# One expert's weights per tile of 128 token slots, with the tokens sorted by expert first, in place of masks over all experts

## The chip, the cores and the metric

The kernel runs on one core of a Trainium2 chip. The metric is device time in microseconds (us), of one launch. The kernel has two parts, one behind the other: attention over 8 sequences (not touched here), and a layer of experts over the same 4,096 tokens.

## The reference, cut to what matters

`x` is the normalised output of the attention, 4,096 rows of 256. There are 8 experts, each token uses the 2 with the highest router value, and the state goes through 2 iterations. (The biases, `mu`, the router and the halting gate are left out of the excerpt where they say nothing new.)

```python
topk_p, topk_i = jax.lax.top_k(probs, K)            # K = 2 of E = 8
v = jnp.zeros_like(xf)
integrated = xf
for _ in range(ITERS):                              # 2
    ctx = jnp.concatenate([integrated, v], axis=-1) # 512 wide
    shared_ctrl = _gelu(ctx @ shared_w1 + shared_b1) @ shared_w2 + shared_b2
    x_sh, v_sh = _inl(shared_ctrl, integrated, v, mu)
    ctrl = _experts(ctx_e, flat_idx, expert_w1, expert_b1, expert_w2, expert_b2)
    x_r, v_r = _inl(ctrl, x_e, v_e, mu)             # one row for each token-expert pair
    ...
    x_next = sw * x_sh + (1.0 - sw) * x_r           # x_r, v_r: weighted sum of the 2 pairs
    v_next = sw * v_sh + (1.0 - sw) * v_r
    halt = jax.nn.sigmoid(_gelu(integrated @ halt_w1 + halt_b1) @ halt_w2 + halt_b2)
    integrated = integrated + halt * (x_next - integrated)
    v = v + halt * (v_next - v)
refined = _gelu(integrated @ refine_w1 + refine_b1) @ refine_w2 + refine_b2
out = layernorm(xf + integration_weight * refined)

def _inl(ctrl, xs, vs, mu):
    a, b, g = jnp.split(ctrl, 3, axis=-1)           # ctrl is 768 wide
    v_next = jax.nn.sigmoid(a) * vs - jax.nn.softplus(b) * (xs - mu)
    return xs + 0.1 * jax.nn.sigmoid(g) * v_next, v_next
```

An expert has a hidden width of 64: 512 -> 64 -> 768. In the first iteration `v` is zero, so only half of the first product and two thirds of the second are needed.

## The kernel before, in words

`experts` works on groups of 512 tokens (4 tiles of 128), 8 groups, two at a time in flight. A stage is one iteration of one group: kinds 1 and 2 are the two iterations, kind 3 is the refinement and the normalisation. A hardware loop runs stages in the order written in `ROUND`: (2, 0), (2, 1), (3, 0), (1, 0), (3, 1), (1, 1), where the second number is the group of the pair. So iterations and refinements of different groups lie beside each other all the time. Every engine has its own instruction stream, and the streams wait for each other on semaphores.

Numbers are kept in float32 precision by splitting each operand in two float16 parts, high and low, and by three products (`split_products`, L1688 to L1690).

In a stage of kind 1 or 2, TensorE turns the state (L1677), computes the router and halting layer (L1728) and the hidden layers of **all** 8 experts and the shared one, for all 512 tokens. One-hot rows of the two chosen experts are spread by TensorE to masks (L1719), and VectorE multiplies the hidden values of all experts by the mask of the first and of the second choice (L1536, `routed`). `control` (L1782) then computes the 768 control values for each tile of 128 tokens and each of 3 streams (the shared expert, the first choice, the second choice). A routed stream takes 13 products over the whole width of 512 hidden values (1 for the bias, 3 for each of 4 chunks), the shared one 2.

ScalarE takes the result out of PSUM: tanh (L1361) and relu (L1363), and later a logarithm (L1348), for which it switches its table and switches back (L1343, L1351). GpSimd makes two products of 128x768 for each tile (L1289, L1291), and VectorE does the rest of `_inl` and the weighted sum (L1544, L1553 to L1569), again for each tile with its 3 streams.

SyncE issues all transfers; in this part they are the weights, the state of each group and the result of each group.

The names that the prediction uses: `control`, `tanhs`, `softplus_logs`, `update`, `low_parts`, `refine_hidden`, `refine_out`, `take_refined`, `refine_variance`, `finish`.

## Time and profile before

| | us |
|---|---|
| median of 3 runs | 1670.16 (1669.14 to 1681.21) |
| the profiled execution: its time | 1671.22 |
| its span | 1669.5 |
| attention, to the first instruction of `experts` at | 594 |
| TensorE busy in the span | 1355.1 (81%) |
| VectorE | 1121.7 (67%) |
| ScalarE | 827.3 (50%) |
| GpSimd | 518.6 (31%) |

The profile's page gives first the busy time of each engine, then the share of busy time in 40 slices, the queues of the transfers, the chain of work that ended last, and the costliest groups of instructions. Attention is the first 14 slices. A matmul's listed duration is its way through a pipeline; what it costs in a row of matmuls is the distance from its start to the start of the next one.

### The profile page before, as it was taken

Reading aid. Unit: us, or ns where it says so; the run is one execution under the profiler, and the core shown is the slowest. Engines: PE = TensorE matmul, PEld = TensorE weight load, DVE = VectorE, ACT = ScalarE, POOL = GpSimd, SP = SyncE. Lnnn points to the kernel's source line nnn. Section 1 sums busy time; section 2 is a strip of 40 time slices with the busy share of each in tenths; the row PEclk is TensorE's granted clock in tenths of the full one; section 3 lists DMA queues with packets and bytes.
Section 4 is the critical chain, followed back from the end, with each engine's and each line's share of the span. In section 5 each row is a group of like instructions: output and inputs, shape, how many; then the busy total and the mean of one; then the engine's idle time right before and its main releaser. Section 6 shows DMA issues by size and latency. Waiting matters only on the chain.

```text
span 1669.5 us, 22624 instructions
## 1 busy us (share of the span) xinstructions
PE 1355.1 (81%) x7776; PEld 726.9 (44%) x7776; DVE 1121.7 (67%) x2038; ACT 827.3 (50%) x1429; POOL 518.6 (31%) x490
## 2 busy tenths in 40 slices
PE   4778877888889827889978789988789987789964
PEld 2334543545445413345533345543345543345532
...
GB/s 83 154 66 122 48 94 105 56 121 56 85 111 19 26 153 1 1 0 1 3 12 26 1 15 1 1 13 26 1 15 1 1 13 11 16 13 1 1 0 26
DMA packets 83216, 62.54 MB, mean 37 GB/s; under 512 B 27633, under 2 KB 82185, under 8 KB 83090
## 3 DMA queue, kind: packets, MB, share of 16 engines
...
q14 instruction: 55, 0.45, 0.1%
...
## 4 chain that ended last, share of the span: by engine, by line
PE 36%; DVE 16%; ACT 5%; issue 4%; SPq 1%; POOL 1%; DMA 1%; POOLq 0%; DVEq 0%; ACTq 0%
PE exp_ps L1782 19%; DVE x L1569 5%; PE exp_ps L1688 4%; PE exp_ps L1690 4%; PE exp_ps L1689 4%; DVE ctrl L1558 2%; PE exp_ps L1677 2%; DVE onehot L1488 2%; PE exp_ps L1728 1%; ACT gp L1338 1%; SPq L1141 1%; PE exp_ps L1719 1%; DVE top_f L1484 1%; DVE sp L1556 1%; DVE ctrl L1553 1%
## 5 line engine op out<-in xcount | busy, mean ns | idle before, releaser
L1782 PE MATMUL exp_ps<-w,routed 128*128 128x512 f16 (+1 forms) x2304 | 442.2, 346 | 1.6 <-DVE routed L1536 1.6
L1289 POOL TENSOR_TENSOR sp<-sp,ctrl 128x768 f32<-128x768 f32 x64 | 124.5, 1945 | 645.4 <-ACT ctrl L1348 645.4
L1782 PEld LDWEIGHTS exp_ps<-w,routed 128*128 128x128 f16 x2304 | 226.7, 99 | 199.8 <-issue 12.2
L563 DVE TENSOR_REDUCE neg_max<-att_ps 128x1 f32<-128x512 f32 (+3 forms) x448 | 216.9, 533 | 71.4 <-PE att_ps L732 69.5
L501 ACT ACTIVATE probs<-att_ps 128x512 f32<-128x512 f32 x320 | 175.5, 609 | 168.3 <-PE att_ps L741 167.3
L1361 ACT ACTIVATE ctrl<-exp_ps 128x512 f32<-128x512 f32 (+1 forms) x192 | 137.2, 715 | 195.3 <-PE exp_ps L1782 194.8
L731 PE MATMUL att_ps<-k_stack,q_stack 96*128 96x512 bf16 (+3 forms) x512 | 161.1, 356 | 69.8 <-DVE neg_max L563 32.5
L1544 DVE TENSOR_SCALAR ctrl<-ctrl 128x768 uint32<-128x768 uint32 x64 | 67.9, 1061 | 125.9 <-ACT ctrl L1361 125.8
L1569 DVE SCALAR_TENSOR_TENSOR x<-ctrl,nwx,x 128x256 f32<-128x256 f32 x192 | 145.7, 759 | 3.4
L741 PE MATMUL att_ps<-q_stack,k_stack 98*128 98x512 bf16 (+3 forms) x512 | 124.6, 317 | 8.3 <-DMA q_stack<-max_parts 5.8
L732 PE MATMUL att_ps<-mask_q,identb 128*128 128x128 bf16 x512 | 125.5, 251 | 0.0
L1291 POOL TENSOR_TENSOR sp<-sp,xm 128x768 f32<-128x768 f32 x64 | 120.8, 1887 | 5.0
L731 PEld LDWEIGHTS att_ps<-k_stack,q_stack 96*128 96x128 bf16 x512 | 54.2, 109 | 143.0 <-DVE neg_max L563 93.9
L1677 PE MATMUL exp_ps<-e_ident,x 128*128 128x128 f32 x192 | 34.4, 330 | 90.2 <-DVE x L1569 56.1
L408 POOL TENSOR_TENSOR wait_carrier<-wait_carrier 128x1 f32<-128x1 f32 x64 | 12.3, 193 | 294.6 <-ACT probs L501 294.6
L1536 DVE TENSOR_TENSOR routed<-gp,masks 128x1024 f16<-128x1024 f16 x128 | 82.8, 688 | 17.3 <-ACT masks L1389 13.9
L1336 ACT ACTIVATE g<-exp_ps,b 128x512 f32<-128x512 f32 x80 | 54.9, 686 | 79.6 <-PE exp_ps L1690 79.5
L413 POOL TENSOR_SCALAR_AFFINE_SELECT probs<-probs 128x640 f32<-128x640 f32 (+2 forms) x192 | 86.6, 483 | 0.0
L1558 DVE SCALAR_TENSOR_TENSOR ctrl<-ctrl,sp 128x768 f32<-128x768 f32 x64 | 76.9, 1202 | 1.1
L798 PE MATMUL att_ps<-probs,values 128*32 128x512 f32 (+3 forms) x1024 | 76.1, 436 | 1.4 <-issue 1.4
L1363 ACT ACTIVATE sp<-exp_ps 128x256 f32<-128x256 f32 x192 | 75.8, 395 | 0.0
L1677 PEld LDWEIGHTS exp_ps<-e_ident,x 128*128 128x128 f32 x192 | 26.2, 168 | 101.8 <-issue 48.9
...
## 6 DMA issues: line engine op xcount, KB each, us to landing
...
x_in<-in_L_attn_encodings SPq DMA_DIRECT2D x8, 512.0 KB, 10.6
normed_dram<-normed SPq DMA_DIRECT2D x8, 512.0 KB, 11.2
x<-normed_dram SPq DMA_DIRECT2D x8, 512.0 KB, 3.9
out<-final SPq DMA_DIRECT2D x8, 512.0 KB, 2.9
ctrl<-in_L_ffn_expert_w SPq DMA_DIRECT2D x1, 1536.0 KB, 8.4
```

The lines of the kernel that those rows point to most:

```text
L501: nc.scalar.activation(probs[:, pair % 4, u, :], src, ACT.Exp).then_inc(free, 1)
L563: return v.tensor_reduce(out, scores, AX.X, ALU.max, negate=True)
L731: t_.matmul(out, stationary, moving, start=True, stop=False)
L732: return t_.matmul(out[:, at:at + P], identb[:], mask, start=False, stop=True)
L741: return t_.matmul(out, k_stack[p][:, h, i * P:(i + 1) * P], q_stack[p][:, h, i * P:TOK], start=True, stop=True)
L1289: gp_.tensor_tensor(sp[:, t], sp[:, t], ctrl[:, t, :, D:2 * D], ALU.subtract).then_inc(pool_step, 1)
L1291: gp_.tensor_tensor(sp[:, t], sp[:, t], xm[:, t, :].unsqueeze(1).to_broadcast([P, STREAMS, D]), ALU.mult).then_inc(spx_ready, 1)
L1361: nc.scalar.activation(ctrl[:, t, s, cols], ctrl_ps(s)[:, 0:width], ACT.Tanh, scale=0.5).then_inc(tanh_done, 1)
L1558: v.scalar_tensor_tensor(gg, gg, 1.0, sp[:, t], ALU.add, ALU.mult).then_inc(update_step, 1)
L1569: last = v.scalar_tensor_tensor(x_new, ctrl[:, t, s, 2 * D:], nwx[g][:, t, s:s + 1], src[g][:, t, :] if s == 0 else x_new, ALU.mult, ALU.add)
L1677: last = t_.transpose(dst[:, t * P:(t + 1) * P], src[:, t, c * P:(c + 1) * P], ident[:])
L1782: last = t_.matmul(ctrl_ps(s)[:, a - cols[0][0]:z - cols[0][0]], stationary, moving[:, a:z], start=(j == 0), stop=(j == len(terms) - 1))
```

## The change

Only `experts` is replaced. What it does now, in the order of its phases:

1. The setup loads all 8 groups' rows at once and keeps the state of all 4,096 tokens in SBUF (`xs`, `vs`). For each group, the router and the shared hidden layer of iteration 1 are computed.
2. The shared expert's control values of iteration 1 (8 groups, units `W_S1`). Beside them: the two choices of each token give 8,192 pairs; VectorE computes for each pair its place in the order of experts, each expert's part padded to whole tiles of 128 slots, 72 tiles (`SLOTS`) in all, 18 units of 4 tiles (`QUADS`). GpSimd scatters each row of `xs` to two places of a DRAM tensor `xs_dram` (64 indirect transfers of 128 rows), which SyncE has filled with zeros before (18 transfers).
3. Iteration 1 of the pairs in 18 units (`W_B`): a unit's rows are loaded from `xs_dram`, each tile uses one expert's weights, whose place TensorE takes from a register that it loads from `tile_expert` (`quad_experts`). The results go to DRAM (`rs1_dram`, 1 MB a unit).
4. Iteration 2 of the shared expert in 8 groups (`W_S2`). Ahead of each, 8 indirect transfers gather the two result rows of each token (`gather1`), and `combine1` adds them to the state. The new state goes to DRAM (`xv_dram`).
5. Iteration 2 of the pairs in 18 units (`W_D`), their rows gathered from `xv_dram` (`gather_state`, 72 indirect transfers of 128 rows of 2 KB), the results stored to `rs2_dram`.
6. The refinement and normalisation of 8 groups, each after 8 indirect transfers (`gather2`) and `combine2`.

A unit has 4 tiles of one stream. `ct` and `rb` have two halves, used in turn (`n % 2`). A routed tile takes 7 products of 128 columns for its hidden layer in iteration 1 and 13 in iteration 2, and 2 products for its control values (the second one carries the low parts and the bias). The diff, cut (`+` of the new kernel, `-` of the old one where it is shown):

```diff
+        GROUPS = SEQS
+        TILES = GROUPS * NT
+        QUADS = 18
+        SLOTS = QUADS * NT
+        XW = D + 4
+        CBW = 2 * 2 * D
+        CBS, CB2S = 6, 8
...
+            sync.wait_ge(zeros_ready, 1)
+            for q in range(QUADS):
+                sync.dma_start(quad_rows(xs_dram, q), zeros[:].unsqueeze(1).to_broadcast([P, NT, XW])).then_inc(pads_zero, 16)
...
+            def load_sorted(q):
+                if q == 1:
+                    sync.wait_ge(ctrl_filled[1], uses(W_B) // 2)
+                if q >= 3:
+                    sync.wait_ge(ew_done, W_B + q - 3 + 1)
+                load(xg_it1(q), quad_rows(xs_dram, q), xg_full[q % 3])
+            def store_results(n, dram, q, width):
+                sync.wait_ge(ew_done, n + 1)
+                sync.dma_start(quad_rows(dram, q), rb[:, n % 2, :, 0:width]).then_inc(rs_stored[n % 2], 16)
+            for g in range(GROUPS):
+                sync.wait_ge(scattered[g], 16 * 2 * NT)
+            for q in range(3):
+                load_sorted(q)
+            for q in range(QUADS):
+                store_results(W_B + q, rs1_dram, q, 2 * D)
+                if q + 3 < QUADS:
...
+            pool.wait_ge(late_in, 16 * LATE)
...
+            pool.wait_ge(pos_ready, 1)
+            pool.wait_ge(pads_zero, 16 * QUADS)
+            for t in range(TILES):
+                for k in range(2):
+                    g_.indirect_dma_start(xs_dram, IndirectOffsetOnAxis(pos[:, 2 * t + k:2 * t + k + 1], 0),
+                                          xs[:, t, :], None).then_inc(scattered[t // NT], 16)
+            def products(n, x):
+                par = n % 2
+                b = ct[:, par, :, D:2 * D] if it_of(n) == 2 else ct[:, par, :, 0:D]
+                m = rb[:, par, :, D:]
+                pool.wait_ge(ln_done, n + 1)
+                g_.tensor_tensor(m, m, b, ALU.subtract).then_inc(pool_step, 1)
+                pool.wait_ge(pool_step, n - W_B + 1)
+                g_.tensor_tensor(m, m, x, ALU.mult).then_inc(mul_done, 1)
+            for q in range(QUADS):
+                products(W_B + q, xg_it1(q)[:, :, 0:D])
+            def gather1(t):
+                if t >= CBS:
+                    pool.wait_ge(comb_done, t - CBS + 1)
+                for k in range(2):
+                    g_.indirect_dma_start(cb1(t)[:, k, :], None, rs1_dram,
+                                          IndirectOffsetOnAxis(pos[:, 2 * t + k:2 * t + k + 1], 0)
+                                          ).then_inc(cb_full[t % CBS], 16)
+            pool.wait_ge(ew_done, W_S2)
+            for i in range(2):
+                pool.wait_ge(rs_stored[i], 16 * stores_before(W_S2, i))
+            for t in range(2 * NT):
+                gather1(t)
+            for g in range(GROUPS):
+                for t in range((g + 2) * NT, min((g + 3) * NT, TILES)):
+                    gather1(t)
+                products(W_S2 + g, xs[:, g * NT:(g + 1) * NT, 0:D])
+            def gather_state(q):
+                if q >= 3:
+                    pool.wait_ge(ew_done, W_D + q - 3 + 1)
                 for t in range(NT):
...
+            for q in range(3):
+                gather_state(q)
+            for q in range(QUADS):
+                products(W_D + q, xg_it2(q)[:, :, 0:D])
+                if q + 3 < QUADS:
+                    gather_state(q + 3)
...
+            def tanhs(n):
+                par, it = n % 2, it_of(n)
+                if n >= 2:
+                    act.wait_ge(ew_done, n - 2 + 1)
+                    if is_shared(n - 2):
+                        act.wait_ge(acc_done, shared_before(n - 2) + 1)
+                    else:
+                        act.wait_ge(rs_stored[par], 16 * (stores_before(n - 2, par) + 1))
+                for u in range(uses(n), uses(n + 1)):
+                    act.wait_ge(ctrl_filled[u % 2], u // 2 + 1)
+                    i = u - uses(n)
+                    if it == 1:
+                        raw = slot_ps(u).rearrange("p (t n) -> p t n", t=2)
+                        last = s.activation(ct[:, par, 2 * i:2 * i + 2, 0:2 * D], raw, ACT.Tanh, scale=0.5)
+                        if u == uses(n + 1) - 1:
+                            last.then_inc(tanh_done, 1)
+                        s.activation(rb[:, par, 2 * i:2 * i + 2, D:], raw[:, :, 0:D],
+                                     ACT.Relu).then_inc(ctrl_freed[u % 2], 1)
+                    else:
+                        raw = slot_ps(u)[:, 0:CTRL]
+                        last = s.activation(ct[:, par, i, :], raw, ACT.Tanh, scale=0.5)
+                        if u == uses(n + 1) - 1:
+                            last.then_inc(tanh_done, 1)
+                        s.activation(rb[:, par, i, D:], raw[:, D:2 * D], ACT.Relu).then_inc(ctrl_freed[u % 2], 1)
+            def logs(n):
+                par = n % 2
+                b = ct[:, par, :, D:2 * D] if it_of(n) == 2 else ct[:, par, :, 0:D]
+                s.preload_act_table_set("natural_log_exp_and_others")
+                act.wait_ge(abs_done, n + 1)
+                s.activation(b, b, ACT.Ln, scale=0.5, bias=half[:, 0:1]).then_inc(ln_done, 1)
+                s.preload_act_table_set("gelu_and_others")
+            act.wait_ge(rf_stored, 32)
+            act.wait_ge(w2_ready, 1)
...
+            def absolute(n):
+                par = n % 2
+                b = (ct[:, par, :, D:2 * D] if it_of(n) == 2 else ct[:, par, :, 0:D]).bitcast(U32)
+                dve.wait_ge(tanh_done, n + 1)
+                v.tensor_scalar(b, b, 0x7FFFFFFF, None, ALU.bitwise_and).then_inc(abs_done, 1)
+            def velocity(n, vel):
+                par = n % 2
+                a, gg, m = ct[:, par, :, 0:D], ct[:, par, :, 2 * D:], rb[:, par, :, D:]
+                dve.wait_ge(mul_done, n - W_B + 1)
+                v.scalar_tensor_tensor(a, a, 1.0, vel, ALU.add, ALU.mult).then_inc(dve_step, 1)
+                then()
+                v.scalar_tensor_tensor(m, a, -10.0, m, ALU.mult, ALU.add).then_inc(dve_step, 1)
+                then()
+                v.scalar_tensor_tensor(rb[:, par, :, 0:D], gg, 1.0, m, ALU.add, ALU.mult).then_inc(ew_done, 1)
...
+            def add_shared1(g):
+                n = W_S1 + g
+                dve.wait_ge(ew_done, n + 1)
+                dve.wait_ge(scattered[g], 16 * 2 * NT)
+                for t in range(NT):
+                    tt = g * NT + t
+                    v.scalar_tensor_tensor(xs[:, tt, 0:D], rb[:, n % 2, t, 0:D], nwx[0][:, tt, 0:1], xs[:, tt, 0:D],
+                                           ALU.mult, ALU.add)
+                    last = v.tensor_scalar(vs[:, tt, :], rb[:, n % 2, t, D:], nwx[0][:, tt, 0:1], None, ALU.mult)
+                last.then_inc(acc_done, 1)
...
+            def combine1(g):
+                for t in range(g * NT, (g + 1) * NT):
+                    dve.wait_ge(cb_full[t % CBS], 32 * (t // CBS + 1))
                     for k in range(2):
...
+            for g in range(GROUPS):
+                if g + 1 < GROUPS:
+                    lows("c", g + 1, 2 * KC)
+                absolute(W_S2 + g)
+                weigh(g)
+                if g + 2 < GROUPS:
+                    combine1(g + 2)
+                if g:
+                    velocity(W_S2 + g - 1, vs[:, (g - 1) * NT:g * NT, :])
+                    add_shared2(g - 1)
+                if g + 1 < GROUPS:
+                    hidden(W_S2 + g + 1, f"cs{g + 1}", h_hl, h_h1)
...
+            for q in range(QUADS):
+                if q + 1 < QUADS:
+                    lows("d", q + 1, 2 * KC)
+                absolute(W_D + q)
+                if q:
+                    velocity(W_D + q - 1, xg_it2(q - 1)[:, :, D:])
+                if q + 1 < QUADS:
+                    hidden(W_D + q + 1, f"dh{q + 1}", h_hl, h_h1)
+            velocity(W_D + QUADS - 1, xg_it2(QUADS - 1)[:, :, D:])
...
+            for g in range(GROUPS):
+                if g:
+                    lows("e", g, KC)
+                    steps = spread_of(g - 1)
+                refine_low(g)
+                if g:
+                    finish(g - 1, steps)
+                take(g)
+                if g + 2 < GROUPS:
+                    combine2(g + 2)
+            finish(GROUPS - 1, spread_of(GROUPS - 1))
         @block.tensor
         def _(pe):
             t_ = nc.tensor
...
+            def control_tile(dst, it, hl, h1, w_at):
+                parts = ((0, 2 * D), (2 * D, CTRL)) if it == 2 else ((D, CTRL),)
+                for j, (stationary, moving) in enumerate(((hl, w2_top), (h1, w2_low))):
+                    for a, z in parts:
+                        last = t_.matmul(dst[:, a - parts[0][0]:z - parts[0][0]], stationary,
+                                         moving[:, ds(w_at + a, z - a)], start=(j == 0), stop=(j == 1))
+                return last
...
-                    else:
-                        k = s - 1
-                        terms = [(onehotT[g][:, k, tok], b2_parts[:])]
-                        for c in range(EC):
-                            terms += [(routed[:, k, 0, c, tok], w2[:, 0, c, :]),
-                                      (routed[:, k, 0, c, tok], w2[:, 1, c, :]),
-                                      (routed[:, k, 1, c, tok], w2[:, 0, c, :])]
-                    for j, (stationary, moving) in enumerate(terms):
...
+            def quad_experts(q):
+                return [pe.value_load(tile_expert[0:1, q * NT + i:q * NT + i + 1], min_val=0, max_val=E - 1)
+                        for i in range(NT)]
+            def routed_hidden(name, chunks, es):
+                dst, done = ring(name)
+                flat = w1[:].rearrange("p a c e r h -> p a c (e r h)")
+                for i in range(NT):
+                    tok = slice(i * P, (i + 1) * P)
+                    o = dst[:, tok]
+                    for c in range(chunks):
+                        hi, lo = flat[:, 0, c, ds(es[i] * P, P)], flat[:, 1, c, ds(es[i] * P, P)]
+                        t_.matmul(o, hi, xT[:, 0, c, tok], start=(c == 0), stop=False)
+                        t_.matmul(o, hi, xT[:, 1, c, tok], start=False, stop=False)
+                        t_.matmul(o, lo, xT[:, 0, c, tok], start=False, stop=False)
+                    last = t_.matmul(o, b1_parts[:, ds(es[i] * P, P)], ones[:], start=False, stop=True)
+                last.then_inc(done, 1)
+            def turn_sorted1(q):
+                pe.wait_ge(xg_full[q % 3], 16 * (q // 3 + 1))
...
+            for q in range(QUADS):
+                if q + 1 < QUADS:
+                    turn_sorted1(q + 1)
+                control(W_B + q, h_hl, h_h1, offsets(es))
+                if q + 1 < QUADS:
+                    es = quad_experts(q + 1)
+                    ready("b", q + 1, KC)
+                    routed_hidden(f"bh{q + 1}", KC, es)
```

## Rows read from the trace of the kernel before

**Rows 1.** Busy time by stretch: attention, experts, the end (header: the columns)

```profile
core 0: us, PE busy (x) PEld busy (x) DVE busy (x) ACT busy (x) POOL busy (x), PEclk, DMA share, GB/s
0.00:594.00 594.00, 470.89 (x3216) 261.26 (x3216) 344.18 (x776) 244.90 (x451) 167.78 (x298) 0.89 0.51 81
594.00:1628.00 1034.00, 866.61 (x4480) 456.04 (x4480) 762.95 (x1217) 569.44 (x958) 339.60 (x187) 0.92 0.04 13
1628.00:1669.50 41.50, 17.58 (x80) 9.65 (x80) 14.61 (x46) 12.96 (x20) 11.20 (x5) 0.66 0.08 26
```

**Rows 2.** Waits, 800 to 1600 us: who waited for whom, total, times, longest

```profile
POOL sp L1289 <- ACT ctrl L1348: 537.8, 26, 30.9
ACT ctrl L1361 <- PE exp_ps L1782: 160.5, 75, 3.2
```

**Rows 3.** Groups by shape, from 740 us: busy us, mean ns; idle before, releaser

```profile
L1782 PE MATMUL exp_ps<-w,routed 128*128 128x512 f16 x1344 | 390.8, 384 | 0.9 <-DVE routed L1536 0.9
L1782 PE MATMUL exp_ps<-w,routed 128*128 128x256 f16 x768 | 209.4, 273 | 0.0
...
L1361 ACT ACTIVATE ctrl<-exp_ps 128x768 f32<-128x768 f32 x96 | 78.6, 819 | 116.1 <-PE exp_ps L1782 116.0
L1363 ACT ACTIVATE sp<-exp_ps 128x256 f32<-128x256 f32 x168 | 66.2, 394 | 0.0
...
L1348 ACT ACTIVATE ctrl<-ctrl,half 128x768 f32<-128x768 f32 x58 | 51.1, 928 | 0.3
L1336 ACT ACTIVATE g<-exp_ps,b 128x512 f32<-128x512 f32 x67 | 46.0, 686 | 71.2 <-PE exp_ps L1690 71.1
L1527 DVE TENSOR_TENSOR gp<-g,gp 128x512 f16<-128x512 f32 x55 | 37.9, 690 | 25.7 <-ACT gp L1338 25.5
L1343 ACT ACT_TABLE_LOAD x29 | 37.2, 1283 | 0.5
L1280 POOL TENSOR_TENSOR xm<-x,mu 128x1024 f32<-128x1024 f32 x14 | 33.3, 2376 | 1.2
L1318 ACT CAST xTp<-exp_ps 128x512 f16<-128x512 f32 x42 | 25.5, 608 | 0.0
```

**Rows 4.** Timeline of VectorE and GpSimd, side by side and alone: start, us

```profile
1077.73 0.96 DVE L1558 SCALAR_TENSOR_TENSOR ctrl<-ctrl,sp 128x768 f32<-128x768 f32 x1
1077.78 2.57 POOL L1289 TENSOR_TENSOR sp<-sp,ctrl 128x768 f32<-128x768 f32 x1 [8.23 <-ACT ctrl L1348]
1078.72 5.81 DVE L1569 SCALAR_TENSOR_TENSOR x<-ctrl,nwx,x 128x256 f32<-128x256 f32 x3
1091.08 1.52 DVE L1569 SCALAR_TENSOR_TENSOR x<-ctrl,nwx,x 128x256 f32<-128x256 f32 x3
```

**Rows 5.** Timeline of TensorE: the same work at either clock, and 128 columns

```profile
1042.07 0.38 PE L1688 MATMUL exp_ps<-xTp,w 128*128 128x512 f16 x1
1042.29 0.38 PE L1689 MATMUL exp_ps<-xTp,w 128*128 128x512 f16 x1
...
1628.11 1.97 PE L1677 MATMUL exp_ps<-e_ident,x 128*128 128x128 f32 x8 [11.99 <-DVE x L1569]
1633.15 0.63 PE L1689 MATMUL exp_ps<-xTp,rf 128*128 128x512 f16 x1
1633.58 0.64 PE L1690 MATMUL exp_ps<-xTp,rf 128*128 128x512 f16 x1
...
441.61 0.22 PE L731 MATMUL att_ps<-k_stack,q_stack 96*128 96x128 bf16 x1
441.66 0.22 PE L732 MATMUL att_ps<-mask_q,identb 128*128 128x128 bf16 x1
```

**Rows 6.** Transfers: median us to landing; then one issue on SyncE's queue

```profile
out<-final SPq DMA_DIRECT2D x8, 512.0 KB, 2.9
ctrl<-in_L_ffn_expert_w SPq DMA_DIRECT2D x1, 1536.0 KB, 8.4
...
609.84 0.43 SPq L1141 DMA_DIRECT2D ctrl<-in_L_ffn_expert_w  x1
```

1589 lines of the change are left out of this document (840 added, 749 removed).

## The prediction

> **What bounds the kernel now.** I read the busy time by stretch first. Experts take 1034 us plus 41.5 us at the end, 1075 of 1669.5; attention, untouched, 594. In the 1034 us TensorE is busy 866.6 us (84%) at a granted clock of 0.92, VectorE 763 (74%), ScalarE 569 (55%), GpSimd 340 (33%) [rows 1]. The waits say the same: GpSimd waits for ScalarE's logarithm, 537.8 us, and ScalarE for TensorE's control products, 160.5 us [rows 2]. By shape, those products are the dearest group (390.8 and 209.4 us listed) and never wait for data [rows 3]. So TensorE is the bound, with VectorE close behind: relief on TensorE alone can't give more than about 1034 - 763 = 271 us.
>
> **What is removed.** Control products fall from 2688 (28 terms a tile, one piece of 512 columns in iteration 1, pieces of 512 and 256 in iteration 2) to 624. Starts of 512 columns are 0.22 us apart at the high clock, 0.43 at the low [rows 5], so it is 481 against 112 us at the high clock. Hidden layers: 720 products of 512 columns (155 us) become 144 of 512 and 1440 of 128 columns, the latter 0.055 us apart (bf16 rows of attention) [rows 5]: 110 us. Masks go, with VectorE's multiplications by them (128 x 0.69 us = 88 us). TensorE loses some 430 us and stops being the bound.
>
> **What isn't removed.** tanh, relu, logarithm and `_inl`: before 32 tiles x 3 streams x 2 = 192 stream-tiles; now 2 x (32 + 72) = 208, because of padding. I therefore cost each phase by the loop that its waits close. Prices for 128x1024 (4 tiles at once): ScalarE 1.0 us from PSUM (0.82 for 768, 0.39 for 256), 0.6 for 512, logarithm 1.15 (0.93 for 768), a table switch 1.28, a GELU 0.6 from start to start, a cast 0.5 [rows 3]; VectorE 1.2 us (0.96 for 768), 0.5 for 256 columns [rows 4], 0.69 for a low part [rows 3]; GpSimd 2.38 [rows 3].
>
> Two prices are chosen. **Contention:** three VectorE instructions on 256 columns take 1.52 us alone, 5.81 us beside GpSimd's products: one gets through per GpSimd instruction [rows 4]. So a pair of products (4.7 us) costs VectorE up to 4.7 us, if two-input work of VectorE falls on it. **An indirect transfer on GpSimd, c:** before has none. The nearest rows are an issue on SyncE, 0.43 us [rows 6], and a GpSimd instruction over 128x1024, 2.38 us [rows 3]. I take the middle, c = 1.4 us for 128 rows. Landing: 2.9 us for 512 KB, 8.4 for 1536 KB [rows 6], so 5.7 for 1 MB and 2.5 for a small one.
>
> **Phase 1, setup and routing, 594 to 768.** VectorE's first low part waits for all late weights. About 10 MB are ahead of that wait; 1.5 MB in 8.4 us is 183 GB/s [rows 6], less its fixed part 200: 50 us, to 645. The first group then carries, in one chain, TensorE 6, ScalarE's cast of 6,912 columns 6, VectorE's low parts of them 8, the ones, bias and refine splits 11, its own hidden layer, turning and routing 14: 45, to 690. Seven more groups: router 3.4 and shared product 2.6 at the low clock, turning 2.0 [rows 5], cast and low part 1.5; between 6.5 and 10.5, I take 8.5: 60. Gates, one-hots, first control and rank products 6, prefix sums and slots (some 35 VectorE instructions of 0.2 to 0.7) 12: 768. The zeros for 9.6 MB take 50 us of transfers, under the routing.
>
> **Phase 2, scatter, to 860.** 64 c = 90 us, 2.5 landing. The shared control units lie under it (VectorE 7.9 a group, 63 in all): `add_shared1` waits for its group's scatter, as it writes the rows that are read. What covers VectorE's work here is the scatter; at small c the 63 us remain.
>
> **Phase 3, 18 units of iteration 1, to 1115.** Load 4 and fill 15. Loop: from one unit's GELU, `hidden` on VectorE 1.0, control of two tiles 1.7 (low clock), 3.2 for tanhs (the second slot comes 1.7 later), switch 1.28, logarithm 1.15, switch 1.28, GELU 1.2: 11.1. `hidden` of the next unit falls on GpSimd's products (they start with the end of the logarithm, last 4.7): plus 2.3 = 13.4; 12.3 at the high clock. I take 13: 17 x 13 = 221. The store (1 MB, 5.7) that `tanhs` two units later waits for gives 11.3, just beneath. Tail 15: logarithm, products, velocity, store.
>
> **Phase 4, iteration 2 of the shared expert, to 1321.** Nothing of it starts before phase 3's last store. First tanhs end after 37: 16 gathers 22.4 + 2.5, combine, turning, 18 products, GELUs, control. Then VectorE is the loop: magnitude 0.9, weights 0.4, `combine1` of 16 instructions 8.2, velocity 3.6, `add_shared2` 2.0, `hidden` 1.0, contention 4, then 7.1 in which it waits for turning, control and four tanhs: 27.2. GpSimd needs 8 c + 4.7 = 16 and hides. 7 x 27.2 less 22 (two groups without combine, one without velocity) = 168; total 206.
>
> **Phase 5, 18 units of iteration 2, to 1621.** Start 37 (logarithm, products, 4 c, turning at the low clock, 52 products, GELU, control). Loop: the gather of 3 units ahead waits for this unit's velocity and stands before the next unit's products, on which the next velocity waits: 3.6 + 4 c + 4.7 + 0.9 contention + 0.2 = 15.0. ScalarE's own loop is 11 to 13.6. What is queued behind GpSimd's wait is thus the products, and VectorE's velocity behind them. 17 x 15 less 6 for the last units = 249, tail 14.
>
> **Phase 6, refinement, to 1856.** First take after 39 (gathers 13.7, turning, 24 and 48 products mostly at the low clock). Before, each refinement lay beside another group's iteration; now a group's is one chain: GpSimd's two products 4.7 with 1 of delay, `combine2` finishing late through contention (to 10 us after `take`), low parts 1.3, variance 2.0, root and switch 1.7, four pairs of GELUs 5.5, low part 0.7, 39 products of 256 columns 4.3: 26. The end of before shows it: from turning at 1628.11 to the span's end is 41 us for one such chain and a half, TensorE at clock 0.66 [rows 1, 5]. 7 x 26 = 182, tail 14.
>
> **The sum:** 594 + 174 + 92 + 255 + 206 + 300 + 235 = 1856 us of span, against 1669.5. The profiled execution's time is 1671.22 and the median 1670.16, 1 us above the span: 1857. So 430 us of TensorE work go, and phases that no longer lie beside each other, their fills, and 264 indirect transfers take more.
>
> No transfer of this trace is issued by GpSimd, so c rests on its two neighbours [rows 3, 6]. The Trainium skill ("DMA: Bandwidth & Descriptors", Anatomy of one DMA, SWDGE path) calls descriptor generation on GpSimd "small, variable", beside about 50 ns of dispatch; by it the sum would be near the first two rivals, 1569 to 1755, by the rows' middle it is 1857. No run here bears the rule out yet.
>
> **Rivals.** (1) *Indirect transfers are nearly free, and ScalarE bounds every loop: faster, 1569.* With c = 0.45 as SyncE's issue, the high clock and no contention: phase 1 150; phase 2 65 (VectorE); phase 3 15 + 170 + 12; phase 4 25 + 7 x 19 less 8; phase 5 30 + 17 x 11 + 12; phase 6 30 + 7 x 20 + 14. That is 975, with attention 1569. For it: the lower price row. Against: the low clock after each idle stretch (8 transposes in 1.97 us) and the contention rows [rows 4, 5]. It decides when the phases behind attention come under 1060 us; c alone can't do it, since it moves at most 64 + 16 + 68 + 8 = 156 us per us, and only down to where ScalarE's loop holds phase 5. (2) *Cheap transfers, else as forecast:* c = 0.75: 1857 - 0.65 x 156 = 1755. (3) *Dear transfers:* c = 2.38: 1857 + 153 = 2010. (4) *TensorE bounds the routed loops.* Each unit loads 4 registers from SBUF between its control and its hidden products, and addresses go through them. No row shows a price: 0 to 1 us each, the latter twice SyncE's issue. Phase 5's TensorE loop at the low clock is 13.6 + 4 loads, above 15 from 0.35 us a load; at 1 us 17.6, phase 3's 15: 17 x (2.6 + 2) = 78, 1935. (5) *The change doesn't do what it says* (an expert overfull, more tiles than 72) is excluded: 8192 pairs need at most 64 + 8 tiles.
>
> **Chances.** Forecast (1790 to 1900) 0.45; (1) 0.07; (2) 0.17; (3) 0.12; (4) 0.17; 0.02 left for no change. A measurement of this kernel tells about 1% from no change. Faster by over 1% 0.07, within 1% 0.02, slower 0.91. The range reaches to most of (2) and half of (3): 1725 to 1985, leaving out (1) and the dear end.
>
> **What would show it.** Right: in the trace after, TensorE's busy share of experts under 60% and a clock under 0.8; four phases with GpSimd's queue filled by transfers; phase 5's units 15 us apart, with the products' wait released by VectorE; refinement groups 26 us apart; nothing routed before 645. Wrong: c far from 1.4; VectorE's instructions of equal length beside GpSimd's products; fills shorter than 30 us.

## The result: 16% slower, and the profile after

The changed kernel takes 1940.25 us (median of 4 runs, 1933.24 to 1948.69) against 1672.58 us (1669.14 to 1681.21) beside it: a ratio of 1.159, 95% interval 1.153 to 1.166. The forecast was 1857 with a range of 1725 to 1985. The time lies inside, 83 us above 1857. That is one phase missed by 95 us, while the errors of the others (19 us too little, 32 too much) go against each other. The profiled execution's span is 1938.2 us, and it is divided below at the forecast's own marks.

First the page of the profile after: busy time of each engine (share of the span, instructions), then the granted clock in 40 slices, in tenths.

```profile
PE 1109.8 (57%) x6930; PEld 680.5 (35%) x6930; DVE 1021.0 (53%) x1930; ACT 870.4 (45%) x1339; POOL 718.1 (37%) x699
...
PEclk9588998989896566657667767766877777767778
```

No engine is busy over 60%. TensorE was at 81% of the span and 1355 us before; it has lost only 245 us of busy time, not the 430 of the forecast's high-clock price. Most of that gap is the clock, which went from 0.9 to 0.759: busy time times granted clock, added up by stretch behind attention, falls by some 355 us (an estimate from [rows 1] and the rows below). The same by stretch, with marks taken from GpSimd's timeline (attention, 594 us, left out); the columns are those of [rows 1]:

```profile
594.00:766.00 172.00, 73.74 (x258) 38.00 (x258) 68.69 (x204) 47.40 (x69) 32.24 (x33) 0.62 0.44 123
766.00:855.00 89.00, 21.02 (x48) 5.91 (x48) 53.98 (x92) 48.86 (x51) 67.92 (x64) 0.58 0.27 96
855.00:1121.00 266.00, 124.20 (x792) 82.60 (x792) 112.88 (x133) 158.37 (x197) 80.89 (x34) 0.71 0.31 100
1121.00:1341.00 220.00, 104.92 (x464) 61.60 (x464) 160.61 (x264) 97.77 (x154) 108.98 (x83) 0.69 0.38 124
1341.00:1714.00 373.00, 205.93 (x1512) 166.35 (x1512) 147.28 (x186) 200.98 (x305) 152.06 (x106) 0.75 0.24 74
1714.00:1938.00 224.00, 108.83 (x640) 65.47 (x640) 133.07 (x278) 71.95 (x113) 108.29 (x82) 0.75 0.28 86
```

One stretch stands out: 1341 to 1714, the 18 routed units of iteration 2. TensorE is busy 55% of it, ScalarE 54%, GpSimd 41%, VectorE 39%. Where [rows 1] had one engine at 84%, here a loop through several engines sets the pace. Who waits in it (waits of the experts' part, 594 to 1938 us: total, times, longest):

```profile
POOL rb L1296 <- ACT ct L1452: 306.8, 29, 23.8
ACT e_xT L1389 <- PE exp_ps L1917: 294.6, 102, 27.1
POOL xg L1327 <- DVE rb L1721: 165.9, 15, 12.5
PE exp_ps L1917 <- DMA xg<-xs_dram: 114.8, 15, 8.0
PE exp_ps L1917 <- DMA xg<-xv_dram,ids: 109.8, 16, 18.6
```

Read the last three together. GpSimd's gather (L1327) waits 15 times for the velocity (L1721) that frees its buffer. Then TensorE's transposes (L1917) wait for the gather's landing, 16 times. The line above shows the same for iteration 1, with SyncE's load in the gather's place. In the view of the kernel before that [rows 2] is taken from, 50 rows long, no wait is on a transfer.

**Forecast and marks, phase by phase.** All marks are starts on GpSimd's queue; "forecast" and "measured" give the stretch's end, and "difference" compares the lengths.

| phase | forecast | measured | difference |
|---|---|---|---|
| 1: setup and routing, to the first scatter | 594 to 768 | 594 to 766.6 | -1 |
| 2 and 3: scatter, 18 units, to the first gather of results | to 1115 | to 1132.8 | +19 |
| 4: shared control, iteration 2, to the first gather of state | to 1329 (1321, then the last logarithm and products) | to 1340.8 | -6 |
| 5: 18 units, to the next gather of results | to 1621 | to 1727.7 | +95 |
| 6: refinement | to 1856 | to 1938.2 | -25 |

### The profile page after: what moved, and what is told of

The parts are those of the page before. It is cut to its first block, busy times and chain, and to the rows that moved or that the text cites. A ratio compares the mean times of both kernels' runs of the same rounds, so it can differ in the third digit from the quotient of the medians.

```text
span 1938.2 us, 21725 instructions
## 1 busy us (share of the span) xinstructions
PE 1109.8 (57%) x6930; PEld 680.5 (35%) x6930; DVE 1021.0 (53%) x1930; ACT 870.4 (45%) x1339; POOL 718.1 (37%) x699
## 4 chain that ended last, share of the span: by engine, by line
DVE 19%; PE 14%; ACT 11%; DMA 10%; issue 9%; POOL 5%; SPq 2%; POOLq 0%; ACTq 0%; DVEq 0%
PE exp_ps L1917 5%; DMA xg<-xs_dram 5%; PE exp_ps L1939 4%; ACT ct L1442 3%; DMA xg<-xv_dram,ids 3%; POOL xg L1327 2%; ACT ct L1435 2%; DVE xs L1847 2%; DVE xs L1781 2%; DVE vs L1782 2%; DVE ct L1710 2%; DVE rb L1721 2%; PE exp_ps L1989 1%; DVE rb L1719 1%; SPq L1122 1%
## 5 line engine op out<-in xcount | busy, mean ns | idle before, releaser
L1917 PE MATMUL exp_ps<-e_ident,xg 128*128 128x128 f32 x432 | 95.0, 405 | 253.2 <-DMA xg<-xs_dram 114.8
L1389 ACT CAST e_xT<-exp_ps 128x512 f16<-128x512 f32 x172 | 97.7, 591 | 295.2 <-PE exp_ps L1917 294.6
L1296 POOL TENSOR_TENSOR rb<-rb,ct 128x1024 f32<-128x1024 f32 x44 | 106.3, 2416 | 307.1 <-ACT ct L1452 306.8
L1551 DVE TENSOR_TENSOR e_xT<-exp_ps,e_xT 128x512 f16<-128x512 f32 x172 | 115.1, 689 | 136.5 <-ACT e_xT L1389 135.7
L1917 PEld LDWEIGHTS exp_ps<-e_ident,xg 128*128 128x128 f32 x432 | 82.8, 216 | 259.7 <-DMA xg<-xs_dram 117.2
L2030 PE MATMUL exp_ps<-e_xT,w 128*128 128x128 f16 x432 | 108.9, 262 | 53.1 <-issue 52.9
L1327 POOL DMA_INDIRECT xg<-xv_dram,ids x72 | 71.4, 991 | 183.1 <-DVE rb L1721 165.9
L1939 PE MATMUL exp_ps<-w_top,h_hl 128*128 (+2 forms) x280 | 102.2, 430 | 37.5 <-DVE h_hl L1558 22.1
L2032 PE MATMUL exp_ps<-e_xT,w 128*128 128x128 f16 x432 | 108.3, 261 | 0.0
L2031 PE MATMUL exp_ps<-e_xT,w 128*128 128x128 f16 x432 | 107.8, 260 | 0.0
L1939 PE MATMUL exp_ps<-w_low,h_h 128*128 (+2 forms) x280 | 98.5, 416 | 0.0
L1442 ACT ACTIVATE ct<-exp_ps 128x768 f32<-128x768 f32 x104 | 84.4, 812 | 13.3 <-PE exp_ps L1939 10.4
L1917 PE MATMUL exp_ps<-e_ident,xs 128*128 128x128 f32 x192 | 32.4, 325 | 99.4 <-DVE vs L1782 68.5
```

Source lines behind the costliest of these rows:

```text
L1327: g_.indirect_dma_start(xg_it2(q)[:, t, :], None, xv_dram, IndirectOffsetOnAxis(ids[:, q * NT + t:q * NT + t + 1], 0)).then_inc(gx_full[q ...
L1442: last = s.activation(ct[:, par, i, :], raw, ACT.Tanh, scale=0.5)
L1551: v.tensor_tensor(xT[:, 1, c, :], ps[:, n % RINGS, :], xT[:, 0, c, :], ALU.subtract).then_inc(ring_freed[n % RINGS], 1)
L1917: last = t_.transpose(dst[:, t * P:(t + 1) * P], tiles(t), ident[:])
L1939: last = t_.matmul(dst[:, a - parts[0][0]:z - parts[0][0]], stationary, moving[:, ds(w_at + a, z - a)], start=(j == 0), stop=(j == 1))
L2030: t_.matmul(o, hi, xT[:, 0, c, tok], start=(c == 0), stop=False)
```

## One unit of phase 5 in the trace after

The unit takes 20.4 us from one pair of products to the next (forecast 15.0). Timeline of the kernel after, one unit, by start; repeated rows left out. Columns: start us, duration us, engine, line, what, and in brackets the idle time before it and what ended it.

```profile
1468.85 1.22 DVE L1721 SCALAR_TENSOR_TENSOR rb<-ct,rb 128x1024 f32<-128x1024 f32 x1
...
1470.34 0.99 POOL L1327 DMA_INDIRECT xg<-xv_dram,ids  x1 [10.85 <-DVE rb L1721]
...
1471.63 0.95 POOL L1327 DMA_INDIRECT xg<-xv_dram,ids  x1 [0.30 <-issue]
...
1473.67 0.69 DVE L1558 TENSOR_TENSOR h_hl<-g,h_hl 64x512 f16<-64x512 f32 x1
1474.13 1.05 POOL L1327 DMA_INDIRECT xg<-xv_dram,ids  x1 [0.30 <-issue]
1475.20 2.35 POOL L1296 TENSOR_TENSOR rb<-rb,ct 128x1024 f32<-128x1024 f32 x1
...
1478.35 3.38 PE L1917 MATMUL exp_ps<-e_ident,xg 128*128 128x128 f32 x16 [6.13 <-DMA xg<-xv_dram,ids]
...
1481.57 0.49 PE L1939 MATMUL exp_ps<-w_top,h_hl 128*128 x2
...
1482.50 0.81 ACT L1442 ACTIVATE ct<-exp_ps 128x768 f32<-128x768 f32 x1
...
1486.40 0.69 DVE L1710 TENSOR_SCALAR ct<-ct 128x1024 uint32<-128x1024 uint32 x1 [3.29 <-ACT ct L1442]
...
1487.01 1.22 DVE L1717 SCALAR_TENSOR_TENSOR ct<-ct,xg 128x1024 f32<-128x1024 f32 x1
```

`hidden`'s low parts are ready at 1474.36, and the control products that use them start only at 1481.57. In between TensorE stands before `turn_sorted2` of the next unit, for 6.13 us, until that unit's gather has landed. That gather could start only after the velocity at 1468.85 to 1470.07. So the loop is: velocity, buffer free, four transfers (1470.34 to 1475.2), landing (1478.35), turning (3.4, at the low clock), control, tanhs (1482.50 to 1486.37), magnitude, velocity (to 1490.75). The working had the gather ahead of the products, which is so (GpSimd's products start at 1475.20). But it let the next velocity wait for those products, and they end at 1479.98, 7 us before that velocity starts: VectorE has the next unit's magnitude (1486.40) ahead of it, and this waits for the tanhs. What the working did not have is the landing and the turning ahead of the control products: it took "3 units ahead" as slack, and one of the three is being turned while another is computed.

## Experiments

Two parts of this reading could fail: another wait might close the same loop, or the loop might be TensorE's own, as the forecast's rival (4) has it. That rival's time, 1935, is nearly the measured one. The first scatter, up to which all the changed kernels run the same code, lies anywhere from 758 to 777 us in their profiled executions, so small differences between medians are read from marks and units inside the traces. **Summary**, differences against the kernel after (1940.25) or, where named, against e9 (1825.26):

| kernel | median us | ratio to before, 95% | difference |
|---|---|---|---|
| e1 seven buffers, phase 5 | 1844.68 | 1.099 to 1.110 | -96 |
| e2 control ahead of turning, phase 5 | 1890.47 | 1.127 to 1.133 | -50 |
| e3 five buffers, phase 3 | 1918.25 | 1.140 to 1.151 | -22 |
| e4 half of the scatter | 1934.72 | 1.152 to 1.163 | -6 |
| e6 no GpSimd products in phase 3 | 1933.56 | 1.152 to 1.159 | -7 |
| e7 buffers and order, both phases | 1899.88 | 1.132 to 1.142 | -40 |
| e8 the same without register loads | 1889.89 | 1.127 to 1.132 | -10 to e7 |
| e9 buffers in both phases | 1825.26 | 1.090 to 1.095 | -115 |
| e10 e9 without register loads | 1826.11 | 1.090 to 1.095 | +1 to e9 |
| e11 e9 with register loads earlier | 1836.78 | 1.092 to 1.102 | +12 to e9 |
| e12 e9 without GpSimd products in phase 3 | 1769.49 | 1.055 to 1.060 | -56 to e9 |
| e5 kernel before, fewer control products | 1604.82 | 0.957 to 0.962 | -67 to before |

### The landing: e1, e3, e9

e1 gives phase 5 seven buffers instead of three (four lie in `vs`, free by then), so a gather runs units ahead of its turning:

```diff
+            if q % 7 >= 3:
+                return view(vs_flat, (q % 7 - 3) * 2048, NT, 2 * D)
...
-                    pool.wait_ge(ew_done, W_D + q - 3 + 1)
+                    pool.wait_ge(ew_done, W_D + max(q - 7 + 1, 0))
```

> Seven buffers in place of three for the rows gathered in iteration 2 (the four new ones lie in vs, which is free by then). Theory A (the buffer's return closes the loop: in the changed kernel's trace a unit's gather waits for the velocity of the unit three before, lands about 8 us later, and only then TensorE turns it, in front of the control products of the unit before): with more buffers nothing waits for the return, a unit goes from 20.5 us to 13.5 to 15, 17 x 6 = 100 us less, about 1840. Theory B (TensorE bounds the unit, by its register loads and the low clock, 13.6 us + 4 loads): a unit stays at 18 us or more, at most 45 us less. Theory C (the rate of the transfers: 4 gathers of 256 KB and a store of 512 KB a unit): no change.

Measured 1844.68, 96 us less. The waits of e1 from 1372 to 1720 us no longer hold a wait of L1919 (there the line of the transposes) on a transfer. In phase 5 the profiled executions, from the first gather of state to the last products, take 373.3 us after and 277.7 in e1, so the 95.6 us between them are the whole miss of that phase. The turning gains too: 16 transposes take 1.94 us in e1 where they took 3.38 behind the wait.

The unit is 14.45 us (products at 1478.48, 1492.95, 1507.41 in e1's timeline) where the forecast had 15.0. The numbers are near, but the loop is another one. GpSimd, whose queue the forecast's 15.0 follows, waits for ScalarE's logarithm in every unit of e1, and the last steps, 14.4 us each, have no gather in them at all:

```profile
POOL rb L1298 <- ACT ct L1454: 74.3, 17, 8.6
...
1575.08 0.95 POOL L1329 DMA_INDIRECT vs<-xv_dram,ids  x1 [0.30 <-issue]
1579.78 2.50 POOL L1298 TENSOR_TENSOR rb<-rb,ct 128x1024 f32<-128x1024 f32 x1 [3.75 <-ACT ct L1454]
...
1594.22 2.51 POOL L1298 TENSOR_TENSOR rb<-rb,ct 128x1024 f32<-128x1024 f32 x1 [8.62 <-ACT ct L1454]
...
1608.64 2.50 POOL L1298 TENSOR_TENSOR rb<-rb,ct 128x1024 f32<-128x1024 f32 x1 [8.62 <-ACT ct L1454]
```

In e1 the chain that repeats goes through TensorE: control products (1470.85 to 1474.82), 2.46 us of idle time, hidden products (1477.28), GELUs (1482.19), copy, low part, and the next control products at 1485.32.

e3 gives phase 3 five buffers for SyncE's load, as each there is half as large:

```diff
-            at = (q % 3) * 2064
+            at = (q % 5) * 1040
...
-                    sync.wait_ge(ew_done, W_B + q - 3 + 1)
+                    sync.wait_ge(ew_done, W_B + q - 5 + 1)
```

> Five buffers in place of three for the sorted rows of iteration 1, nothing else. Theory A: the same loop, through SyncE's load (issue to landing 6.0 us) in place of the gather: a unit goes from 14.4 us to 12.5 to 13, 17 x 1.7 = 29 us less, about 1911. Rival: contention of VectorE with GpSimd's products, or the store of 1 MB, closes the loop: no change within 10 us.

Measured 1918.25: 22 us less (phases 2 and 3 together take 347.2 us instead of 366.1). Units fall from 14.36 to 13.2 us; the forecast took 13. Two rows of the kernel after show what stood there: the load is issued when the velocity is done, and lands in front of the transposes.

```profile
991.65 0.51 SPq L1122 DMA_DIRECT2D xg<-xs_dram  x1
...
997.73 1.97 PE L1917 MATMUL exp_ps<-e_ident,xg 128*128 128x128 f32 x8 [7.49 <-DMA xg<-xs_dram]
```

e9 has both edits.

> The kernel after, with five buffers for phase 3's loads and seven for phase 5's gathers; order as in the kernel after. The landing theory: the two gains (95 and 22 us) stand in different phases and add, so about 1822 us (1812 to 1835). Rival: the two phases share something (a buffer, a queue), and the sum is 1835 to 1850.

Measured 1825.26, 115 us less: the two gains add, to within 3 us of the 118 that they make apart.

### Another order instead of more buffers: e2, e7

If landing and turning are ahead of the control products, one could let the control products go first. e2 does so in phase 5, on all three engines:

```diff
-                if q + 1 < QUADS:
-                    turn_sorted2(q + 1)
                 control(W_D + q, h_hl, h_h1, offsets(es))
                 if q + 1 < QUADS:
+                    turn_sorted2(q + 1)
```

and in the same way `casts` after `tanhs` on ScalarE and `lows` after `absolute` on VectorE.

> Three buffers as in the changed kernel, but in iteration 2 of the pairs the control products of a unit stand before the turning of the next one on TensorE, with the casts behind the tanhs on ScalarE and the low parts behind the magnitude on VectorE. Theory A: the gather may land late, since control no longer waits for it; a unit is then closed by velocity 3.7 + gathers 4.8 + products 4.8 + some waiting = 14 to 15 us, about 1840, within 20 us of the run with seven buffers. Theory B: 18 us or more a unit, above 1890. If buffers alone matter and not the order, no change.

Measured 1890.47: half of the gain, with units of 16.6 us, between what the two theories asked for. The expectation missed what the old order hid: in e2 the hidden products wait 2.83 us for low parts. e7 shows it with the landing out of the way (this order and the deep buffers in both phases):

> The changed kernel with seven and five buffers and with control before turning in both iterations of the pairs. Theory A: units of 11.5 to 13 us in iteration 1 and 12 to 14 in iteration 2: 1940 - 17 x 1.9 - 17 x 7.3 = 1784, between 1770 and 1820. It stays above the kernel before, since setup, scatter and the fills between the phases are not touched. Theory B: above 1850.

Measured 1899.88, 75 us more than e9 with the same buffers and 116 above the middle of what was expected. A unit of phase 5 takes 17.9 us in e7 against 14.45, one of phase 3 14.3 against 13.2. e7's timeline of one unit:

```profile
1466.99 0.82 PE L1941 MATMUL exp_ps<-w_top,h_hl 128*128 x2 [3.34 <-DVE h_hl L1560]
...
1468.57 0.81 ACT L1444 ACTIVATE ct<-exp_ps 128x768 f32<-128x768 f32 x1 [3.80 <-PE exp_ps L1941]
...
1472.82 2.06 ACT L1391 CAST e_xT<-exp_ps 128x512 f16<-128x512 f32 x4
1473.44 2.48 DVE L1553 TENSOR_TENSOR e_xT<-exp_ps,e_xT 128x512 f16<-128x512 f32 x4
1474.90 1.28 ACT L1452 ACT_TABLE_LOAD   x1
...
1476.28 0.23 PE L2032 MATMUL exp_ps<-e_xT,w 128*128 128x128 f16 x1 [2.73 <-DVE e_xT L1553]
```

The casts (2.06 us) now lie between the tanhs and the table switch, on ScalarE's chain, and the hidden products wait 2.73 us for low parts made behind them. In the old order both lay beside TensorE's idle time before the control products. So the wait that the order removed was the cover of other work, and what was late next was that work.

e7's unit of phase 5 is also 1.3 us longer than e2's, though it has more buffers. In e2 the gathers, which wait for the velocity, hold GpSimd's products back, and VectorE's copy of the hidden values (L1557) takes 0.29 us. In e7 the products start as the logarithm ends, and the same copy (L1559) takes 1.45 us beside them (means from 1400 to 1540 us).

### Register loads on TensorE, the forecast's rival (4): e8, e10, e11

Each unit has four `value_load` of expert numbers on TensorE between control and hidden products. In e1 TensorE is idle there, with nothing named:

```profile
1477.28 0.23 PE L2032 MATMUL exp_ps<-e_xT,w 128*128 128x128 f16 x1 [2.46 <-issue]
```

e8 and e10 take constants in their place, over e7 and e9; what they leave out is that each tile gets its own expert's weights:

```diff
-                return [pe.value_load(tile_expert[0:1, q * NT + i:q * NT + i + 1], min_val=0, max_val=E - 1)
-                        for i in range(NT)]
+                return [(q * NT + i) % E for i in range(NT)]
```

e11 keeps the loads and puts them ahead of turning:

```diff
+                this = offsets(es)
                 if q + 1 < QUADS:
+                    es = quad_experts(q + 1)
                     turn_sorted2(q + 1)
-                control(W_D + q, h_hl, h_h1, offsets(es))
+                control(W_D + q, h_hl, h_h1, this)
                 if q + 1 < QUADS:
-                    es = quad_experts(q + 1)
```

> As the run before it, but TensorE takes constants in place of the expert numbers loaded to registers (tile i uses expert i mod 8), so that each pair gets some expert's values and not its own: the register loads and computed addresses are gone. Theory A (hidden behind ScalarE's logarithm): within 15 us of the run before it. Theory B (they are on TensorE's path, about 2.5 us a unit as the trace of the changed kernel shows before L2030): 17 x 2 x 2.5 = 85 us less.

> As the kernel with both buffers deeper, and the experts' numbers are constants (slot tile i takes expert i mod 8), so TensorE loads no registers; the routed outputs are then of the wrong experts, by intent. In the trace with seven buffers TensorE stands 2.46 us idle, issue named, between the control products and the hidden products of every unit of phase 5, with nothing else late. Theory of the register loads: they are that gap and close the unit of 14.45 us, which falls to about 12; 17 units of 2.4 us less: about 1780 us (1770 to 1795). Rival: another engine closes the unit as soon (ScalarE is busy 10.9 us of it, VectorE 10.6), and less than 12 us come off.

> As the kernel with both buffers deeper, and TensorE loads the registers of the next unit ahead of turning it rather than behind this unit's control products; nothing is left out. TensorE waits 1.26 us for the low parts of the hidden sums there, so of 2.46 us of loads about 1.2 remain: 17 units of about 1.2 us less, about 1800 us (1793 to 1812). Rival (loads cost nothing): the same as with both buffers deeper within 5 us.

Measured: e8 1889.89 (10 us less than e7), e10 1826.11 (1 us more than e9), e11 1836.78 (12 more). As the price of a unit rival (4) is out: it asked for 78 us. The expectations of e10 (40 us less) and of e11 (25 less) both failed. The gap is gone in e10, and it lay on the chain that repeats in e1; but the unit of phase 5 grew from 14.45 to 15.35 us (15.1 and 15.6 in turn), while that of phase 3 fell from 13.2 to 13.1. One view says where the gain went: VectorE's groups by shape, 1400 to 1600 us (line, shape, count | busy, mean ns | idle before). In e1, whose phase 5 is built as e9's:

```profile
L1559 DVE COPY h_h<-h_hl 64x512 f16<-64x512 f16 x14 | 14.7, 1051 | 18.5 <-ACT h_hl L1406 18.5
```

In e10, and then in e11:

```profile
L1559 DVE COPY h_h<-h_hl 64x512 f16<-64x512 f16 x13 | 31.5, 2421 | 0.0
L1559 DVE COPY h_h<-h_hl 64x512 f16<-64x512 f16 x13 | 31.7, 2440 | 0.0
```

The copy needs 0.28 us alone. In e10 ScalarE's GELUs no longer wait for the hidden products (2.5 us in e1), so the copy starts 3.5 us after GpSimd's first product instead of 4.9, in the middle of the second, and is held until that ends: 1.05 us became 2.42. What the missing loads gave, contention took back. TensorE then waits 3.7 us for `hidden`, 2.4 more than in e1, and its granted clock from 1400 to 1600 us falls from 0.90 to 0.82.

e11's trace shows both at once, and its loss lies in phase 5 alone (301 us against 291 in e9, units of 14.4 to 15.4 us; phase 3 keeps its 13.2). The idle gap has moved with the loads and stands ahead of the transposes. And as ScalarE's GELUs no longer wait for hidden products there either, the copy is held as long as in e10, 2.44 us.

```profile
1438.13 3.17 PE L1919 MATMUL exp_ps<-e_ident,xg 128*128 128x128 f32 x16 [2.52 <-issue]
```

How the 10 us divide between the two was not separated.

### VectorE beside GpSimd's products: e6, e12

The forecast priced contention from [rows 4] and put 2.3 us of it into phase 3's unit. e6 takes GpSimd's two products of that phase over 4 of the 256 columns of each tile (16 of 1024 in a unit), in the kernel after; e12 does the same in e9. Both leave most of the routed velocities of iteration 1 unscaled:

```diff
+                if it_of(n) == 1:
+                    m, b, x = m[:, :, 0:4], b[:, :, 0:4], x[:, :, 0:4]
```

> The changed kernel with GpSimd's two products a unit in iteration 1 of the pairs on 4 of 256 columns, so that part of the result is left out: two instructions of 2.4 us become short. GpSimd is idle 9.7 us of each unit there. Theory E (contention: VectorE's h_hl instruction takes 2.73 us beside the products, 0.69 alone): it is 0.69 again and the time falls by up to 18 x 2.0 = 36 us, less if the landing of the load closes the loop instead (14.4 us a unit stays): 0 to 36. Rival (an idle engine's work is free): under 5 us, and the h_hl instruction stays at 2.7.

> As the kernel with both buffers deeper, and GpSimd's two products of a unit of phase 3 are taken over 4 columns of 1024, so most of the routed velocities of iteration 1 keep their unscaled values. With three buffers the landing of the load covered this. With five buffers the unit took 13.2 us, with the hidden sums' low parts held for 2.73 us instead of 0.69. Theory of contention: those 2.0 us are on the loop, the unit falls to about 11.2, 17 units: 34 us less than with both buffers deeper, about 1788 us (1780 to 1798). Rival: VectorE's instruction is held for nothing that counts, and less than 8 us come off.

Measured: e6 1933.56, 7 us less; e12 1769.49, 56 us less than e9, more than the 27 to 45 that were expected. The 7 us of e6 lie at the ends of phase 3 (its first and last steps are 11.2 us for 13.2, and its last products short); the 15 steps between take 217.6 us against 217.7. The same edit is worth eight times as much once the landing is out of the loop. In both the held instruction is freed. VectorE's groups from 880 to 1090 us, e9:

```profile
L1560 DVE TENSOR_TENSOR h_hl<-g,h_hl 64x512 f16<-64x512 f32 x16 | 43.8, 2736 | 0.2
```

and e12:

```profile
L1562 DVE TENSOR_TENSOR h_hl<-g,h_hl 64x512 f16<-64x512 f32 x18 | 12.4, 689 | 0.3
```

That is 2.05 us a unit, but the unit fell by 2.9, from 13.2 to 10.3 us (17 of them: 49 us; the last unit's own two products, 4 us, are the rest of 53 between marks). The part above 2.05 fits the clock: TensorE's control products (128x512) wait for this instruction, and after the longer wait they run slower. TensorE's groups from 900 to 1080 us, e9:

```profile
L1941 PE MATMUL exp_ps<-w_top,h_hl 128*128 x56 | 34.8, 622 | 81.2 <-DVE h_hl L1560 81.2
```

and e12:

```profile
L1943 PE MATMUL exp_ps<-w_top,h_hl 128*128 x64 | 27.3, 427 | 33.7 <-DVE h_hl L1562 33.7
```

622 ns is the low clock of 1.2 GHz throughout, in the group shown and in that of `w_low`; 427 is mostly the high one (0.38 us each at starts 0.22 apart, in e12's timeline, against 0.63 and 0.43). TensorE waited 81.2 us for `hidden` over 14 units in e9, 33.7 over 16 in e12. So a late VectorE instruction cost more than its own lateness: in e9 the first tanh starts 2.0 us after the first control product, in e12 1.15, and these 0.85 us are what 2.9 has over 2.05.

The Trainium skill ("SBUF — State Buffer", Who interferes with whom) says that VectorE and GpSimd share a port pair as a lock, which a VectorE instruction with two inputs in SBUF, or a copy in one of its fast modes, needs while GpSimd reads: whoever comes second is fully held until the first has finished. The traces agree: the low part's instruction takes 0.69 us alone, 2.73 when it starts 0.24 us into a product of 2.42 us, and it ends 0.55 us after that product. GpSimd's product is held in turn: 2.35 us in the kernel after, 3.22 in e9's phase 5, where it starts beside the third velocity instruction.

### Scatter and TensorE's relief: e4, e5

e4 leaves out the second choice of every token in the scatter, 32 of 64 transfers:

```diff
-                for k in range(2):
+                for k in range(1):
...
-                sync.wait_ge(scattered[g], 16 * 2 * NT)
+                sync.wait_ge(scattered[g], 16 * NT)
```

> Only the first choice of each token is scattered (32 indirect transfers in place of 64); the rows of the second choice are left as zeros, so that part of the result is left out. Theory A (the scatter is on the path at its pace of 1.3 us a transfer, until the shared units on VectorE, some 63 us, take over): 20 to 30 us less, about 1915. Rival (the shared units cover the scatter): under 5 us less. If all 32 transfers counted it would be 42 us.

Measured 1934.72: 6 us less, where 20 to 30 were expected, near the rival's "under 5". In e4 the last scatter starts at 811.6 instead of 852.8, but the first products come at 862.52 instead of 877.59. What stands there is the shared control units on VectorE, every 9.65 us (timeline of e4):

```profile
817.65 0.48 DVE L1745 SCALAR_TENSOR_TENSOR xs<-rb,nwx,xs 128x256 f32<-128x256 f32 x1
...
827.30 0.49 DVE L1745 SCALAR_TENSOR_TENSOR xs<-rb,nwx,xs 128x256 f32<-128x256 f32 x1
...
836.95 0.48 DVE L1745 SCALAR_TENSOR_TENSOR xs<-rb,nwx,xs 128x256 f32<-128x256 f32 x1
```

So the forecast's phase 2 was rightly put at the longer of scatter and shared units, and the two are nearer to each other than it said (VectorE 63 us of work, but spread over eight units that each also go through ScalarE: 77). Of the 17 us gained between first scatter and first products 7 were lost again in phase 5, whose gathers took 4.5 us to land instead of 4.0; e4's empty slots are rows of zeros with the id 0, so more than half of the rows gathered there are row 0, and whether they land later for that wasn't tried.

e5 leaves 9 of 13 control products of the routed streams out of the kernel before, to see how far TensorE's work alone carries there:

```diff
-                        for c in range(EC):
+                        for c in range(1):
```

> The kernel before, with 9 of the 13 control products of each routed stream left out (hidden chunks 1 to 3 don't reach the result): 1728 of 2688 products, some 310 us of TensorE at the high clock; nothing else is changed. Theory D (the kernel before is bound by TensorE with VectorE close behind, at 763 busy us of 1034): 150 to 250 us less, 1420 to 1520, VectorE over 85% busy in the experts. Rival (waits between the engines set the time, TensorE's busy share is only high): under 80 us less.

Measured 1604.82, 67 us less, for 266 us of TensorE's busy time (1355 to 1089). The expectation was 150 to 250; the rival, that waits between the engines set the time, had under 80, and that is what came. Stretch 800 to 1560 us of the kernel before and then of e5, columns as in [rows 1]:

```profile
800.00:1560.00 760.00, 657.87 (x3403) 346.84 (x3402) 569.33 (x933) 425.64 (x724) 251.44 (x126) 0.92 0.03 9
```

```profile
800.00:1560.00 760.00, 476.69 (x2235) 244.31 (x2232) 615.51 (x974) 448.02 (x758) 276.50 (x135) 0.80 0.03 9
```

VectorE, at 75% before, is at 81%; TensorE falls to 63%, and its clock from 0.92 to 0.80. The limit of 271 us that the forecast gave was an upper bound from VectorE's busy time, and a quarter of it is what came. The waits in the same stretch say who was next, before and then in e5:

```profile
PE exp_ps L1677 <- DVE x L1569: 35.2, 12, 6.4
```

```profile
PE exp_ps L1677 <- DVE x L1569: 168.7, 13, 15.4
```

TensorE's turning (L1677) now waits for the end of VectorE's update of the state.

## Why the prediction was right, and where it wasn't

**Direction: right, and the cause in the main.** The forecast said that relief of TensorE does not carry over, since phases stand one behind another and each is closed by a loop through several engines. The traces have it: TensorE is busy 48% of the 1344 us behind attention (638.6, the forecast said under 60%), at a clock of 0.58 to 0.75 by stretch (under 0.8), and e5 shows that even without new phases the relief is worth 67 us. The premise "So TensorE is the bound, with VectorE close behind" does not hold as it stands: with 266 us of TensorE's busy time gone the kernel before gets 4% faster, so waits between the engines hold it as well, and TensorE's busy share alone does not say what its relief is worth.

**Phase 1: right**, within 1.4 us, which is closer than it repeats (758 to 777 us in the profiled executions). VectorE's work on the late weights starts at 641.1 us (forecast 645), and nothing is routed before. Its smaller terms were not each measured.

**c, the indirect transfer: right.** 63 steps between 766.63 and 852.79 us are 1.37 us each (forecast 1.4); most are 1.26, 0.96 busy and 0.30 between. The gathers are nearer to 1.3 (1.27 and 1.28 us on average):

```profile
L1327 POOL DMA_INDIRECT xg<-xv_dram,ids x72 | 71.4, 991 | 183.1 <-DVE rb L1721 165.9
L1287 POOL DMA_INDIRECT xs_dram<-xs,pos x64 | 67.9, 1061 | 126.1 <-DVE pos L1703 106.9
...
xg<-xv_dram,ids POOLq DMA_INDIRECT x72, 4.0
...
xs_dram<-xs,pos POOLq DMA_INDIRECT x64, 2.5
```

The middle of SyncE's issue and a GpSimd instruction [rows 3, 6] was a lucky choice, but it had two sides to be held against. Rivals (1), (2) and (3) fall with it. The rule of the Trainium skill that the prediction weighed ("DMA: Bandwidth & Descriptors", Anatomy of one DMA, SWDGE path: descriptor generation "small, variable") doesn't hold as the price of 128 rows, if this busy time is that work: 0.96 to 1.06 us on average in each group.

**Phase 3: the unit was mis-sized**, 14.36 us against 13. The 13 were the loop through ScalarE with contention, and e3, with the load out of the way, has units of 13.2. (The working's terms, 1.0 + 1.7 + 3.2 + 1.28 + 1.15 + 1.28 + 1.2, add up to 10.8, not to its 11.1, and e12 has 10.1 in most units without the contention.) The forecast looked for a rival loop in the *store* (11.3 us), and didn't look for the one through the *load*: velocity, load (6.0 us to land, by the page of the profile), turning, control. 17 x 1.36 = 23 us too little for the units; the scatter's end 4 us early gives some back, and 19 are left.

**Phase 4: right**, 208 us between marks against 214 (units of about 25 us against 27.2).

**Phase 5: the step that failed**, 387 us against 292. The sum "3.6 + 4c + 4.7 + 0.9 + 0.2" is a loop along GpSimd's queue: velocity, four gathers, products, "on which the next velocity waits". That last link never closes a unit: in the kernel after the velocity starts 7 us behind the products' end, held by the magnitude. e1's 14.45 us are another loop, through TensorE, so that they lie within 4% of 15.0 is luck. The step skipped is in "the gather of 3 units ahead waits for this unit's velocity": who waits for *that* gather was asked only on GpSimd's queue. The consumer on the other side, turning on TensorE, stands ahead of the next control products, and landing (4.0 us, median) and turning (3.4 us at the low clock) are in the loop. With them the unit is 20.4, and 17 x 5.4 = 92 us.

**Phase 6: 25 us too much**, as the groups are 24.0 us apart (forecast 26), 14 us over seven, and the rest in start and tail.

**Contention: right in kind, wrong in what it is worth.** One VectorE instruction gets through per GpSimd product, 2.73 us against 0.69. But it costs hardly anything beside the landing (e6: 7 us) and 56 us without it (e12), of which part fits TensorE's clock; a fixed "plus 2.3" belongs only in the loop that closes.

**Rival (4): near in time, false in cause.** 1935 was forecast for register loads of 1 us, 1940 was measured, and taking all loads away gives 10 us (e8) or none (e10). Both were tried with the deep buffers only; with three, TensorE waits some 6 us for a landing in each unit of phase 5. Had only the total been read, this would have passed for the explanation.

**What stays open.** How e11's loss divides between the moved gap and the held copy. What the units of e1 and e9 would take with loads and contention both gone: no run has that. Whether the order of e2 can be had without moving the casts and low parts: not tried. No form of the changed kernel beats the one before; the nearest with all work in it, e9, is 9% slower, and even e12, with work left out, 5.7%.
